# Cross attention scores: from pairs of 64-row products to eight products of 32 rows by 64 columns, two chunks at a time

## The chip, the cores and the metric

The kernel runs on one core of one Trainium2 chip. The metric is the device time of one execution in microseconds (us); the time before is the median of three runs. "PE" is TensorE's matmul side, "PEld" its weight load, DVE is VectorE, ACT ScalarE, POOL GpSimd, SP SyncE.

## The reference

Three residual layers on x (8 batches, 64 rows, 512 features):

```python
x = x + xattn(layernorm(x), ctx)   # 16 heads of 32; ctx is 8 x 1601 x 512
x = x + attn(layernorm(x))         # 8 query heads, one key/value head, causal
x = x + ffn(layernorm(x))          # 2 shared experts, top 2 of 8 routed ones

# xattn, where the change is:
q = query @ Wq.T + bq; k = ctx @ Wk.T + bk; v = ctx @ Wv.T + bv
scores = einsum('bhqd,bhkd->bhqk', q, k) / sqrt(32)
s = where(scores >= 0, scores + 1, 1 / (1 - scores))
out = einsum('bhqk,bhkd->bhqd', s / s.sum(-1), v) @ Wo.T + bo
```

All is computed to fp32 accuracy; the large products split each operand into a high and a low part of a faster type (`wkh`, `wkl`, `cxh`, `cxl`) and add three products.

## The kernel before

Everything is one program, with the order of the work on each engine written out by hand as a loop over slots, and a semaphore for each kind of hand-over. The first 104 slots (`NCH`) are the cross attention: each of the 8 batches has 1601 context rows, cut into 13 chunks (`PER`) of 128 rows, the last of 65; six parts of 256 rows, the last of 321, are the units in which the context is loaded (SP, `load_ctx`), split (ACT `context_hi`, POOL `context_lo`) and turned into keys.

What TensorE does in slot n, in this order (loop at the end of `pe`): steps of the self attention for the two batches just finished, called a tile (t = 0 to 3, steps d = 0 to 14, placed by `slot_of`); `scores(n)`; `attended`, a tile step; `weighted(n - 1)`; `denominators` where a batch is done; two of the four `keys(i, g)` of the next part (one or none in the last slots of a batch); `values(n + 2)`. Keys, values and tile steps share two PSUM banks in turn: `take` waits until the use before the last one has been read out (`proj_read`, counted in the order of `projections()`).

- `scores(n)`, line 692: the query's heads are in `qb`, spread so that 64 rows hold two heads and their columns are zero where the head is the other one. For each g of 4 (four heads) and j of 2 one fp32 product: 64 rows of keys times 128 columns of `qb`, into bank `scb[n % 2][j]`. Two pairs of banks (2 and 3, 4 and 5) take turns, so `scores(n)` waits for the weights of chunk n-2 (`f_dve`).
- ACT turns the scores s into Exp(-Ln(1 + Relu(-s))), two instructions of 512 columns each (lines 1110, 1115, 1119); DVE adds Relu(s) (`weights`, line 1225), which gives the stablemax weight in `tt`, one of `TR` = 3 buffers.
- `weighted(n)`, line 706: 16 fp32 products of 32 columns of values (`va`, one of `VR` = 3 buffers, copied by DVE in `values`, line 1220) and 64 columns of weights, four side by side in four strips of columns.
- POOL adds the weights of each chunk into `dacc` (line 528), from which `denominators` sums over rows.

DVE runs through the same slots in this order: the values copy of the slot before, tile steps, `denominators`, the early `keys` read-outs (line 1212), `weights(n, 0)` and `weights(n, 1)`, the late `keys` read-outs, `normalised`, and in the last slots `weights_split` (line 1320; low parts of the FFN's weights, after ACT's `weights_hi`, line 1068). `weights_hi(1)` and `weights_split(1)` stand at slot 103; the first waits for the last values product (`v_pe`), since its target lies over memory of the cross attention.

From slot 104 on the shared experts run, `shared_up` and `shared_down` (lines 849, 868), then the routed ones (lines 984, 1001). The steps 12 to 14 of tile 2 stand in slots 104 to 106, those of tile 3 begin in slot 106.

## Time and profile before

| | us |
|---|---|
| median of 3 runs (1334.54 to 1336.66) | 1334.65 |
| the profiled execution | 1335.17 |
| its span | 1333.5 |
| PE busy | 1314.2 |
| DVE busy | 657.4 |
| ACT busy | 643.4 |
| POOL busy | 408.6 |
| PE's instructions (matmul records) | 12136 |

The span is what the instructions cover; the execution's own time is 1.67 us more. A matmul's duration in the records overlaps that of its neighbours, since matmuls are pipelined: the distance from start to start is what one costs. Each fp32 product appears as two records of its line (two passes), each split product (keys, values) as one.

### The profile page before, as it was taken

How to read it: one execution, taken by the hardware profiler on the slowest of the kernel's cores; microseconds unless marked ns; L12 is line 12 of the kernel's file. 1: busy time of each engine (PE TensorE's matmuls, PEld its weight loads, DVE VectorE, ACT ScalarE, POOL GpSimd, SP SyncE). 2: the span in 40 equal slices, each digit the busy share in tenths (PEclk: the TensorE clock that was granted, in tenths of full speed). 3: DMA queues.
4: the chain of work that ended last, by engine and by line, in shares of the span. 5: the costliest groups of instructions: out<-in, count | busy, mean ns of one | idle time of the engine just before them, and what ended most of it. 6: DMA issues, size and time to landing. Idle time of an engine off the chain costs nothing.

```text
span 1333.5 us, 28096 instructions
## 1 busy us (share of the span) xinstructions
PE 1314.2 (99%) x12136; PEld 1135.2 (85%) x12136; DVE 657.4 (49%) x979; ACT 643.4 (48%) x1125; POOL 408.6 (31%) x213
## 2 busy tenths in 40 slices
PE   9999999999999999999999999799999999999997
PEld 6888888888788888888889888688988999999896
DVE  5334433534443443443353454656674555455555
ACT  4455545435454543635543644546554354454443
POOL 2344344444354443444444443400013000010000
PEclk9999999999999999999999999899999999999999
DMA  6221111121111111121121130655545389999990
GB/s 215 87 74 32 34 37 33 32 68 49 59 50 33 49 68 49 33 76 32 34 68 65 47 130 21 247 176 186 174 169 185 138 331 337 366 337 335 360 388 34
DMA packets 34868, 174.71 MB, mean 131 GB/s; under 512 B 6154, under 2 KB 8362, under 8 KB 18484
## 3 DMA queue, kind: packets, MB, share of 16 engines
q1 hardware_dynamic: 32996, 168.10, 34.7%
q0 software_dynamic: 1744, 4.76, 1.2%
q8 instruction: 98, 1.61, 0.5%
q14 instruction: 30, 0.25, 0.1%
HBM read 166.78 MB, written 6.06 MB: 130 GB/s over the span
## 4 chain that ended last, share of the span: by engine, by line
PE 96%; DVE 2%; ACT 1%; DMA 1%; POOL 1%; issue 0%; PEldq 0%; SPq 0%; DVEq 0%; PEld 0%; ACTq 0%
PE bank L662 22%; PE bank L674 21%; PE bank L984 11%; PE bank L1001 8%; PE po L868 6%; PE bank L849 6%; PE po L706 4%; PE po L692 4%; PE bank L692 4%; PE bank L766 1%; PE bank L730 1%; PE bank L811 1%; DMA xres<-in_x 1%; PE po L826 1%; PE bank L826 1%; DVE wsl L1320 0%
## 5 line engine op out<-in xcount | busy, mean ns | idle before, releaser
L528 POOL TENSOR_TENSOR xn<-xn,tt 128x1024 f32<-128x1024 f32 x96 | 230.0, 2396 | 406.7 <-DVE tt L1225 406.7
L662 PE MATMUL bank<-cxh,wkh 128*128 128x256 f32 (+1 forms) x752 | 225.9, 300 | 1.1 <-DVE xa L1295 1.1
L1320 DVE TENSOR_TENSOR wsl<-ring,wsh 128x2048 fp32r<-128x2048 f32 x72 | 167.8, 2331 | 114.9 <-ACT wsh L1068 114.7
L662 PE MATMUL bank<-cxl,wkh 128*128 128x256 f32 (+1 forms) x752 | 215.8, 287 | 0.0
L662 PE MATMUL bank<-cxh,wkl 128*128 128x256 f32 (+1 forms) x752 | 214.8, 286 | 0.0
L1212 DVE TENSOR_SCALAR kk<-bank,bkt 128x256 f32<-128x256 f32 (+1 forms) x190 | 93.4, 492 | 241.0 <-PE bank L662 239.9
L674 PE MATMUL bank<-wvh,cxh 128*128 128x512 f32 (+1 forms) x416 | 164.5, 396 | 0.0
L674 PE MATMUL bank<-wvl,cxh 128*128 128x512 f32 (+1 forms) x416 | 163.8, 394 | 0.0
L674 PE MATMUL bank<-wvh,cxl 128*128 128x512 f32 (+1 forms) x416 | 162.7, 391 | 0.0
L1068 ACT CAST wsh<-ring 128x2048 fp32r<-128x2048 f32 x72 | 137.2, 1906 | 47.8 <-PE po L868 24.2
L1110 ACT ACTIVATE tt<-bank 128x512 f32<-128x512 f32 (+1 forms) x104 | 56.5, 595 | 208.6 <-PE bank L692 208.6
L1110 ACT ACTIVATE tt<-po 128x512 f32<-128x512 f32 (+1 forms) x104 | 56.5, 595 | 203.5 <-PE po L692 203.5
L1220 DVE COPY va<-bank 128x512 f32<-128x512 f32 (+1 forms) x104 | 71.7, 689 | 166.9 <-PE bank L674 166.9
L662 PEld LDWEIGHTS bank<-cxh,wkh 128*128 128x128 f32 x752 | 141.7, 188 | 12.8 <-issue 2.9
L984 PEld LDWEIGHTS bank<-xT,ring 128*128 128x128 f32 x1280 | 144.8, 192 | 1.0
L984 PE MATMUL bank<-xT,ring 128*128 128x128 f32 x1280 | 144.8, 275 | 0.0
L662 PEld LDWEIGHTS bank<-cxh,wkl 128*128 128x128 f32 x752 | 142.2, 189 | 0.0
L662 PEld LDWEIGHTS bank<-cxl,wkh 128*128 128x128 f32 x752 | 141.8, 189 | 0.0
L1115 ACT ACTIVATE tt<-tt 128x512 f32<-128x512 f32 (+1 forms) x208 | 119.8, 631 | 0.4
L1119 ACT ACTIVATE tt<-tt 128x512 f32<-128x512 f32 (+1 forms) x208 | 119.3, 627 | 0.0
L514 POOL TENSOR_TENSOR cxl<-ctxt,cxh 128x1024 fp32r<-128x1024 f32 (+1 forms) x47 | 108.5, 2308 | 17.0 <-ACT cxh L1027 17.0
L674 PEld LDWEIGHTS bank<-wvh,cxl 128*128 128x128 f32 (+1 forms) x416 | 76.4, 184 | 20.0
(242 smaller groups left out, 2196.3 us busy)
## 6 DMA issues: line engine op xcount, KB each, us to landing
ring<-in_w SPq DMA_DIRECT2D x112, 1024.0 KB, 6.3
ctxt<-in_ctx SPq DMA_DIRECT2D x40, 512.0 KB, 3.5
ctxt<-in_ctx SPq DMA_DIRECT2D x8, 642.0 KB, 3.9
wqt<-in_wo SPq DMA_DIRECT2D x4, 1024.0 KB, 6.6
wqt<-in_aq SPq DMA_DIRECT2D x4, 1024.0 KB, 7.3
wqt<-in_ap_ SPq DMA_DIRECT2D x4, 1024.0 KB, 6.4
yrows<-K SPq DMA_DIRECT2D x1, 2048.0 KB, 8.9
tt<-in_wk SPq DMA_DIRECT2D x2, 512.0 KB, 5.3
```

The costliest lines, as they stand in the source:

```text
L514: e.tensor_tensor(lo, src, hi.bitcast(F32), ALU.subtract).then_inc(s["cl_pool"], 1)
L528: e.tensor_tensor(dacc[0:kn, y, :], dacc[0:kn, y, :], tt[0:kn, w, :], ALU.add).then_inc(s["da_pool"], 1)
L662: m = e.matmul(dst[:, 0:n], (wkh, wkl)[a][:, c, g * P:(g + 1) * P], (cxh, cxl)[b][:, u, c, 0:n], start=(c == 0 and x_ == 0), stop=(c == 3 ...
L674: m = e.matmul(dst[0:kn, :], (cxh, cxl)[a][:, u, c, k * P:k * P + kn], (wvh, wvl)[b][:, c, :], start=(c == 0 and x_ == 0), stop=(c == 3 an ...
L692: m = e.matmul(scb[n % 2][j][0:kn, P * g:P * g + P], kk[r, u, g, k * P:k * P + kn], qb[r, b % 2, g, :], start=True, stop=True)
L984: m = e.matmul(bank[q % 2][:, P * jj:P * jj + P], ring[slot(un)][:, 512 * c + P * jj:512 * c + P * jj + P], xg[:, y, c, :], start=(c == 0) ...
L1001: m = e.matmul(bank[2][:], h_[:, j, :], w_[r_ % 3][:, 512 * jj:512 * jj + 512], start=(j == 0 and x_ == 0), stop=(j == 15 and x_ == 2))
L1068: e.copy(wsh[m % 3][:], ring[slot(un)][:]).then_inc(s["wh_act"], 1)
L1110: e.activation(tt[0:kn, w, 512 * hb:512 * hb + 512], scb[n % 2][hb][0:kn, :], ACT.Relu, scale=-1.0).then_inc(s["t_act"], 1)
L1115: e.activation(tt[0:kn, w, r], tt[0:kn, w, r], ACT.Ln, bias=1.0).then_inc(s["ln_act"], 1)
L1119: e.activation(tt[0:kn, w, r], tt[0:kn, w, r], ACT.Exp, scale=-1.0).then_inc(s["ex_act"], 1)
L1320: e.tensor_tensor(wsl[m % 3][:], ring[slot(unit_split(m))][:], wsh[m % 3][:].bitcast(F32), ALU.subtract).then_inc(s["wl_dve"], 1)
```

## The change

- `scores` is made of products of 32 rows (one head): the stationary operand is 64 of the chunk's key columns, the moving one the head's 64 query columns straight from `qc`. Eight products (two halves of the chunk, four heads) stand on eight separate tiles of the array; head h writes into bank 2 + h. The last chunk of a batch, 65 rows, is not halved. `qb` with its fill and its copies (`queries`) is gone.
- Chunks go in pairs (`group`): in even slots of a batch both chunks' scores are made, then the weighted sums of the pair before; the 13th chunk is alone. Both chunks' scores share the banks 2 to 5, so a pair waits for the weights of all chunks before it. ACT begins when both chunks of a pair are there (`s_pe`, now one count a chunk). DVE makes the first chunk's weights before the late keys and the second's after them.
- `VR` and `TR` are 4. `tt` holds the heads in the order of the banks, and `weighted` and `denominators` read it so.
- Tile steps stand one slot later; the steps 12 and 13 of tile 2 come to slots 96 and 97. Step 14 stays in slot 104.
- `values` of chunks 101 to 103 move to the slots 101 to 103 (before: 99, 101 and 102). `shared_up(0)` moves from slot 104 to slot 102 and writes into bank 6; `weighted(103)` is first in slot 104.

The diff, without the hunks that only drop `qb`, follow the new banks or move `iota512`:

```diff
@@ -28,8 +28,8 @@
 NPART = NPT * NB
 PER = 13
 NCH = PER * NB
-VR = 3
-TR = 3
+VR = 4
+TR = 4
 NR = 8
 NBLK = 15
 NSH = 16
...
@@ -105,9 +105,9 @@
 
     if t == 3:
         return NCH + 2 + LAST_TILE[d]
-    if t == 2 and d >= 12:
-        return NCH + d - 12
-    return 2 * PER * t + 2 * PER + 5 + (9 if d == 10 else d)
+    if t == 2 and d == 14:
+        return NCH
+    return 2 * PER * t + 2 * PER + 6 + (9 if d == 10 else d)
 
 
 def tile(slot, d):
...
@@ -122,9 +122,30 @@
 
 def values_in(slot):
 
-    if slot + 2 < NCH - 2:
+    if slot + 2 < NCH - 3:
         return slot + 2
-    return slot + 1 if NCH - 2 <= slot + 1 < NCH else None
+    return slot if NCH - 3 <= slot < NCH else None
+
+
+def group(slot):
+
+    if not 0 <= slot < NCH or slot % PER % 2:
+        return ()
+    return (slot, slot + 1) if slot % PER < PER - 1 else (slot,)
+
+
+def group_of(n):
+
+    return group(n) or group(n - 1)
+
+
+def group_before(slot):
+
+    if slot == NCH:
+        return group(NCH - 1)
+    if not group(slot) or slot == 0:
+        return ()
+    return group(slot - 2) or group(slot - 1)
 
 
 def projections():
...
@@ -152,9 +173,10 @@
         def sb(name, shape, dt=F32):
             return st.enter_context(nc.sbuf_tensor(name, shape, dt))
 
-        bank = [st.enter_context(nc.psum_tensor(f"bank{i}", [P, 512], F32)) for i in range(4)]
-        po = st.enter_context(nc.psum_tensor("po", [P, 2048], F32))
-        bank += [po[:, 512 * i:512 * i + 512] for i in range(4)]
+        bank = [st.enter_context(nc.psum_tensor(f"bank{i}", [P, 512], F32)) for i in range(2)]
+        sc = st.enter_context(nc.psum_tensor("sc", [P, 4, 512], F32))
+        bank += [sc[:, i, :] for i in range(4)]
+        bank += [st.enter_context(nc.psum_tensor(f"bank{i}", [P, 512], F32)) for i in range(6, 8)]
 
         ident = sb("ident", [P, P])
         mask = sb("mask", [P, 64])
...
@@ -306,10 +327,13 @@
         pj = [bank[0], bank[1]]
         uses = projections()
         use = {u: n for n, u in enumerate(uses)}
-        scb = (bank[2:4], bank[4:6])
         pob = bank[6:8]
         three = ((0, 0), (0, 1), (1, 0))
 
+        def up_bank(s_):
+
+            return bank[2 + s_ % 2] if s_ else bank[6]
+
         def unit_shared(s_, kind):
 
             return 2 * (s_ // 2) + kind
...
@@ -336,9 +360,13 @@
 
 
 
-        def weights_of(buffer, g, h):
-            c0 = 512 * (h // 2) + 128 * g + 64 * (h % 2)
-            return buffer[:, c0:c0 + 64]
+
+        def score_read(n, kn, hb):
+            c0 = 256 * (n - group_of(n)[0])
+            return sc[0:kn, 2 * hb:2 * hb + 2, c0:c0 + 256]
+
+        def weights_view(n, kn, hb):
+            return tt[0:kn, n % TR, 512 * hb:512 * hb + 512].rearrange("p (h c) -> p h c", h=2)
 
         def ctx_views(i):
             n, u = width(i), i % 2
...
@@ -432,7 +460,6 @@
             e.wait_ge(s["da_pool"], NCH)
             for n in range(5, 8):
                 load_shared(n)
-            store_rows(2)
             for n in range(8, 32):
                 if n == 23:
                     store_rows(3)
...
@@ -677,22 +703,21 @@
 
             def scores(n):
                 i, k, kn = chunk(n)
-                u, b = i % 2, i // NPT
-                if n % PER == 0:
-                    e.wait_ge(s["qb_act"], 4 * b + 4)
+                u, b, c0 = i % 2, i // NPT, 256 * (n - group_of(n)[0])
                 if n >= 2:
-                    e.wait_ge(s["f_dve"], 2 * (n - 2) + 2)
+                    e.wait_ge(s["f_dve"], 2 * group_of(n)[0])
                 else:
                     e.wait_ge(s["q_act"], 4)
                 for g in range(4):
                     if k == 0:
                         e.wait_ge(s["proj_read"], use["k", i, g] + 1)
-                    for j in range(2):
-                        r = slice(64 * j, 64 * j + 64)
-                        m = e.matmul(scb[n % 2][j][0:kn, P * g:P * g + P], kk[r, u, g, k * P:k * P + kn],
-                                     qb[r, b % 2, g, :], start=True, stop=True)
-                        if g == 3:
-                            m.then_inc(s["s_pe"], 1)
+                    for y0, y1 in ((0, 64), (64, P)) if kn == P else ((0, kn),):
+                        for h in range(4):
+                            r = slice(32 * h, 32 * h + 32)
+                            m = e.matmul(sc[y0:y1, h, c0 + 64 * g:c0 + 64 * g + 64],
+                                         kk[r, u, g, k * P + y0:k * P + y1], qc[r, g, 64 * b:64 * b + 64],
+                                         start=True, stop=True)
+                m.then_inc(s["s_pe"], 1)
 
             def weighted(n):
                 kn, b = chunk(n)[2], n // PER
...
@@ -705,8 +730,8 @@
                     for h in range(4):
                         m = e.matmul(pob[b % 2][32 * h:32 * h + 32, 64 * g:64 * g + 64],
                                      va[0:kn, n % VR, P * g + 32 * h:P * g + 32 * h + 32],
-                                     weights_of(tt[0:kn, n % TR, :], g, h), start=(head and g == 0),
-                                     stop=(tail and g == 3), skip_group_check=True)
+                                     tt[0:kn, n % TR, 256 * h + 64 * g:256 * h + 64 * g + 64],
+                                     start=(head and g == 0), stop=(tail and g == 3), skip_group_check=True)
                 m.then_inc(s["p_pe"], 1)
 
             def denominators(b):
...
@@ -835,14 +859,16 @@
                     e.wait_ge(s["wl_dve"], un + 1)
                 if s_ >= 2:
                     e.wait_ge(s["ge_act"], s_ - 1)
+                elif s_ == 1:
+                    e.wait_ge(s["f_dve"], 2 * NCH)
                 else:
-                    e.wait_ge(s["f_dve"], 2 * (NCH - 1))
+                    e.wait_ge(s["cr_dve"], normalised_by(NB - 2))
                 if r == 0:
                     e.wait_ge(s["xl_pool"], 2 + p)
                     if p == 1:
                         e.wait_ge(s["xl_dve"], 1)
                 for i in range(2):
-                    dst, k_ = bank[2 + s_ % 2][:, 256 * i:256 * i + 256], 0
+                    dst, k_ = up_bank(s_)[:, 256 * i:256 * i + 256], 0
                     col = 256 * (s_ % 2) + 128 * i
                     for c in range(4):
                         for w_, x_ in ((wsh, xh), (wsh, xl), (wsl, xh)):
...
@@ -927,21 +953,23 @@
                     turn_third(tile(n, 13))
                 if tile(n, 14) is not None:
                     gate(tile(n, 14))
-                if n < NCH:
-                    scores(n)
+                for m in group(n):
+                    scores(m)
                 if tile(n, 9) is not None:
                     for b in range(2):
                         attended(tile(n, 9), b)
-                if NCH <= n < NCH + 2 * NSH:
+                for m in group_before(n):
+                    weighted(m)
+                if NCH < n < NCH + 2 * NSH:
                     shared_up(n - NCH)
-                if 1 <= n < NCH + 1:
-                    weighted(n - 1)
                 for b in finished(n)[0]:
                     denominators(b)
                 for i, g in early + late:
                     keys(i, g)
                 if values_in(n) is not None:
                     values(values_in(n))
+                if n == NCH - 2:
+                    shared_up(0)
                 if n == PLACE:
                     positions()
                 if n == PLACE + 2:
...
@@ -1056,7 +1075,7 @@
             def split_hi(t):
                 e.wait_ge(s["proj_read"], use["t3", t] + 1)
                 if t == 2:
-                    e.wait_ge(s["d_pe"], NB)
+                    e.wait_ge(s["v_pe"], NCH)
                 e.copy(xh[t // 2][:, :, P * (t % 2):P * (t % 2) + P], xaT[:]).then_inc(s["xh_act"], 1)
 
             def weights_hi(m):
...
@@ -1096,33 +1115,30 @@
                 e.wait_ge(s["q_pe"], g + 1)
                 e.activation(qc[:, g, :], bank[(6, 7, 2, 3)[g]][:], ACT.Identity, bias=bqs[:, g:g + 1],
                              scale=XSCALE).then_inc(s["q_act"], 1)
-            for h in range(4):
-                queries(0, h)
 
             for n in range(NSLOT):
-                if n < NCH:
-                    w, kn = n % TR, chunk(n)[2]
-                    if n >= TR:
-                        e.wait_ge(s["da_pool"], n - TR + 1)
-                        e.wait_ge(s["p_pe"], n - TR + 1)
+                for m in group(n):
+                    kn = chunk(m)[2]
+                    if m >= TR:
+                        e.wait_ge(s["da_pool"], m - TR + 1)
+                        e.wait_ge(s["p_pe"], m - TR + 1)
+                    e.wait_ge(s["s_pe"], group(n)[-1] + 1)
                     for hb in range(2):
-                        e.wait_ge(s["s_pe"], 2 * n + hb + 1)
-                        e.activation(tt[0:kn, w, 512 * hb:512 * hb + 512], scb[n % 2][hb][0:kn, :], ACT.Relu,
+                        e.activation(weights_view(m, kn, hb), score_read(m, kn, hb), ACT.Relu,
                                      scale=-1.0).then_inc(s["t_act"], 1)
+                for m in group(n):
+                    w, kn = m % TR, chunk(m)[2]
                     for hb in range(2):
                         r = slice(512 * hb, 512 * hb + 512)
-                        e.wait_ge(s["t_act"], 2 * n + hb + 1)
+                        e.wait_ge(s["t_act"], 2 * m + hb + 1)
                         e.activation(tt[0:kn, w, r], tt[0:kn, w, r], ACT.Ln, bias=1.0).then_inc(s["ln_act"], 1)
                     for hb in range(2):
                         r = slice(512 * hb, 512 * hb + 512)
-                        e.wait_ge(s["ln_act"], 2 * n + hb + 1)
+                        e.wait_ge(s["ln_act"], 2 * m + hb + 1)
                         e.activation(tt[0:kn, w, r], tt[0:kn, w, r], ACT.Exp, scale=-1.0).then_inc(s["ex_act"], 1)
                 for i in range(2, NPART):
                     if first(i - 1) - 2 == n:
                         context_hi(i)
-                b, h = divmod(n + 5, PER)
-                if 0 < b < NB and h < 4:
-                    queries(b, h)
                 if tile(n, 0) is not None:
                     root(1, tile(n, 0))
                 for half in range(2):
...
@@ -1220,10 +1236,9 @@
                 e.tensor_copy(va[0:kn, n % VR, :], pj[use["v", n] % 2][0:kn, :]).then_inc(s["proj_read"], 1)
 
             def weights(n, hb):
-                kn, w, r = chunk(n)[2], n % TR, slice(512 * hb, 512 * hb + 512)
+                kn, t_ = chunk(n)[2], weights_view(n, chunk(n)[2], hb)
                 e.wait_ge(s["ex_act"], 2 * n + hb + 1)
-                e.scalar_tensor_tensor(tt[0:kn, w, r], scb[n % 2][hb][0:kn, :], 0.0, tt[0:kn, w, r], ALU.max,
-                                       ALU.add).then_inc(s["f_dve"], 1)
+                e.scalar_tensor_tensor(t_, score_read(n, kn, hb), 0.0, t_, ALU.max, ALU.add).then_inc(s["f_dve"], 1)
 
             def stats_of(l, t):
                 e.bn_stats(stats[:, t, :], xres[:, t, :]).then_inc(s["bn_dve"], 1)
...
@@ -1532,11 +1547,14 @@
                     denominators(b)
                 for i, g in early:
                     keys(i, g)
-                if n < NCH:
-                    weights(n, 0)
-                    weights(n, 1)
+                for m in group(n)[:1]:
+                    weights(m, 0)
+                    weights(m, 1)
                 for i, g in late:
                     keys(i, g)
+                for m in group(n)[1:]:
+                    weights(m, 0)
+                    weights(m, 1)
                 for b, g, m in finished(n)[1]:
                     normalised(b, g, m)
 
```

## Rows read from the trace of the kernel before

**Rows 1.** The page: span, its part 1 (busy time, share, instructions) and the granted clock.
```profile
span 1333.5 us, 28096 instructions
PE 1314.2 (99%) x12136; PEld 1135.2 (85%) x12136; DVE 657.4 (49%) x979; ACT 643.4 (48%) x1125; POOL 408.6 (31%) x213
PEclk9999999999999999999999999899999999999999
```

**Rows 2.** The page's part 4: chain of waits, by engine, then by line.
```profile
PE 96%; DVE 2%; ACT 1%; DMA 1%; POOL 1%; issue 0%; PEldq 0%; SPq 0%; DVEq 0%; PEld 0%; ACTq 0%
PE bank L662 22%; PE bank L674 21%; PE bank L984 11%; PE bank L1001 8%; PE po L868 6%; PE bank L849 6%; PE po L706 4%; PE po L692 4%; PE bank L692 4%; PE bank L766 1%; PE bank L730 1%; PE bank L811 1%; DMA xres<-in_x 1%; PE po L826 1%; PE bank L826 1%; DVE wsl L1320 0%
```

**Rows 3.** Busy time in one stretch, all engines; granted clock, DMA share and rate at the end.
```profile
36.80:848.60 811.80, 809.96 (x8829) 688.17 (x8828) 354.60 (x613) 401.42 (x762) 359.61 (x163) 1.00 0.16 53
```

**Rows 4.** Timeline of TensorE in one slot: start, duration, engine, line, names, count.
```profile
401.44 0.40 PE L674 MATMUL bank<-wvl,cxh 128*128 128x512 f32 x1
401.67 0.39 PE L674 MATMUL bank<-wvh,cxl 128*128 128x512 f32 x1
401.99 1.16 PE L692 MATMUL po<-qb,kk 64*128 64x128 f32 x16
403.08 0.65 PE L706 MATMUL po<-tt,va 128*32 128x64 f32 x32
403.67 0.42 PE L662 MATMUL bank<-cxh,wkh 128*128 128x322 f32 x1
403.92 0.31 PE L662 MATMUL bank<-cxl,wkh 128*128 128x322 f32 x1
404.07 0.32 PE L662 MATMUL bank<-cxh,wkl 128*128 128x322 f32 x1
```

**Rows 5.** Groups of instructions by line: fp32 passes of 512, 128 and 8 moving columns.
```profile
L811 PE MATMUL bank<-wqt,xa 128*128 128x512 f32 x32 | 14.4, 592 | 0.0
L766 PE MATMUL bank<-xaT,wqt 128*128 128x128 f32 x128 | 14.9, 275 | 0.0
L743 PE MATMUL bank<-rwt,xaT 128*128 128x8 f32 x32 | 3.8, 246 | 0.0
```

**Rows 6.** Timeline of TensorE: first and last of 24 key products, first values.
```profile
396.40 0.28 PE L662 MATMUL bank<-cxl,wkh 128*128 128x256 f32 x1
396.52 0.28 PE L662 MATMUL bank<-cxh,wkl 128*128 128x256 f32 x1
...
398.89 0.28 PE L662 MATMUL bank<-cxl,wkh 128*128 128x256 f32 x1
399.01 0.28 PE L662 MATMUL bank<-cxh,wkl 128*128 128x256 f32 x1
399.13 0.40 PE L674 MATMUL bank<-wvh,cxh 128*128 128x512 f32 x1
399.37 0.39 PE L674 MATMUL bank<-wvl,cxh 128*128 128x512 f32 x1
```

**Rows 7.** Timeline of ScalarE and VectorE behind the scores of single chunks.
```profile
397.80 1.15 ACT L1119 ACTIVATE tt<-tt 128x512 f32<-128x512 f32 x2
398.45 1.29 DVE L1225 SCALAR_TENSOR_TENSOR tt<-bank,tt 128x512 f32<-128x512 f32 x2
...
402.10 0.69 DVE L1220 COPY va<-bank 128x512 f32<-128x512 f32 x1 [1.96 <-PE bank L674]
403.27 1.09 ACT L1110 ACTIVATE tt<-po 128x512 f32<-128x512 f32 x2 [4.32 <-PE po L692]
404.24 1.15 ACT L1115 ACTIVATE tt<-tt 128x512 f32<-128x512 f32 x2
405.28 1.15 ACT L1119 ACTIVATE tt<-tt 128x512 f32<-128x512 f32 x2
```

**Rows 8.** Groups of instructions of GpSimd: sums of weights, split of the context.
```profile
L528 POOL TENSOR_TENSOR xn<-xn,tt 128x1024 f32<-128x1024 f32 x96 | 230.0, 2396 | 406.7 <-DVE tt L1225 406.7
L514 POOL TENSOR_TENSOR cxl<-ctxt,cxh 128x1024 fp32r<-128x1024 f32 (+1 forms) x47 | 108.5, 2308 | 17.0 <-ACT cxh L1027 17.0
```

**Rows 9.** The page's part 3: the queue that fetches instructions.
```profile
q8 instruction: 98, 1.61, 0.5%
```

**Rows 10.** Timelines and granted clock where the stretch ends.
```profile
847.16 0.28 PE L849 MATMUL bank<-xAh,wsl 128*128 128x256 f32 x1
848.06 0.65 PE L706 MATMUL po<-tt,va 65*32 65x64 f32 x32 [0.62 <-DVE tt L1225]
...
847.02 1.89 ACT L1068 CAST wsh<-ring 128x2048 fp32r<-128x2048 f32 x1
854.83 1.09 PE L750 MATMUL bank<-ident,xa 128*128 128x128 f32 x4 [6.12 <-POOL xa L540]
855.93 0.41 PE L849 MATMUL bank<-xAl,wsh 128*128 128x256 f32 x1
856.15 0.41 PE L849 MATMUL bank<-xAh,wsl 128*128 128x256 f32 x1
859.94 0.28 PE L849 MATMUL bank<-xAh,wsh 128*128 128x256 f32 x1
860.06 0.28 PE L849 MATMUL bank<-xAl,wsh 128*128 128x256 f32 x1
852.80:859.50 6.70, 4.67 (x22) 4.70 (x23) 3.89 (x4) 0.04 (x1) 1.89 (x1) 0.50 1.02 410
853.85 2.28 DVE L1320 TENSOR_TENSOR wsl<-ring,wsh 128x2048 fp32r<-128x2048 f32 x1
```

**Rows 11.** Groups of instructions that the change takes away from ScalarE and GpSimd.
```profile
L1036 ACT COPY qb<-qc 32x256 f32<-32x256 f32 x32 | 12.9, 403 | 0.6
L508 POOL MEMSET qb<- 128x1024 f32 x1 | 1.0, 952 | 0.1
```

More of the change, by code:

```diff
@@ L716, in denominators @@
                     e.wait_ge(s["unit_pool"], 1)
-                dv = dacc[:, b % 2, :].rearrange("p (j g e q) -> p j g e q", j=2, g=4, e=2)
                 for h in range(4):
-                    m = e.matmul(dst[32 * h:32 * h + 32, 0:256], unit[:], dv[:, h // 2, :, h % 2, :], start=True,
-                                 stop=True)
+                    m = e.matmul(dst[32 * h:32 * h + 32, 0:256], unit[:], dacc[:, b % 2, 256 * h:256 * h + 256],
+                                 start=True, stop=True)
                 m.then_inc(s["d_pe"], 1)
@@ L1210, in keys @@
                 if i >= 2 and g == 0:
-                    e.wait_ge(s["s_pe"], 2 * (first(i - 2) + chunks_of(i - 2)))
+                    e.wait_ge(s["s_pe"], first(i - 2) + chunks_of(i - 2))
                 e.tensor_scalar(kk[:, u, g, 0:n], key_bank(i, g)[:, 0:n], bkt[:, g:g + 1], None,
```

18 lines of the change are left out of this document (4 added, 14 removed).

## The prediction

> **What bounds the kernel now.** The page comes first: TensorE is busy for 1314.2 of 1333.5 us at the granted clock 1.0 almost throughout, the other engines for half of the span or less [rows 1]. The profiled execution took 1335.17 us (1.67 beside its span), 0.52 above the median of 1334.65. The chain of waits says the same: PE 96%, the scores (L692) 8%, the weighted sums (L706) 4% [rows 2]. So what counts is TensorE's order of work. The change touches it from 36.8 to 848.6 us, where PE is busy for 809.96 of 811.80 us [rows 3]: there a stall is nearly absent, and every instruction slot saved is time saved unless a new wait eats it.
>
> Next the timeline of one slot [rows 4]. Scores run from 401.99 to 403.08 (1.09 us, 16 passes: each fp32 product is two), weighted sums to 403.67 (0.59 us, 32 passes), then keys. Three times in a slot TensorE changes the form of its tiles, and each change shows as a gap beyond the regular pitch. Values to scores: 0.32 against 0.23 for its neighbours, so 0.09. In the scores the last pass starts 1.16-0.27 = 0.89 after the first; seven later pairs and a late second one make the pitch 0.112, eight pitches 0.90, and 0.19 is left. In the sums 0.65-0.22 = 0.43 lies between first and last start; with the late second group the pitch is 0.056, eight make 0.45, and 0.14 is left. The second key product starts 0.25 after the first against 0.15: 0.10. Together 0.52 us for a round of form changes.
>
> **The change part by part.** (1) *Scores.* Removed per chunk: 8 pairs of passes, 64 rows, 128 columns loaded, 128 moving. Added: 32 products of 32 rows, 64 loaded, 64 moving, in groups of eight on eight separate tiles; 8 groups of passes again (4 head groups, two passes). Nothing in the trace has eight tiles. What sets a pass is read from neighbours: 512 moving columns cost (14.4/4-0.592)/7 = 0.43 us, so 64 cost 0.054; 8 moving columns behind a 128-column load cost (3.8/4-0.246)/7 = 0.10, so a load sets its own pace of about 0.8 ns a column, 64 columns 0.05 [rows 5]. The old pair runs two 128-column loads in 0.112, so loads of different rows run together; the old sums run four 32-column loads in 0.056 where one after another would be 0.10, so loads of different column strips overlap at least by two, and eight tiles need just that [rows 4]. Starts inside a group lie about 7 ns apart (the sums: four tiles, 32 passes in 0.43 us with room left in each 0.056), and eight times 7 is 0.056. All three limits meet at 0.056; I take 0.058 for the group of eight, 0.46 us a chunk against 0.90. The 65-column last chunk of a batch has four tiles and a 65-column load: the same 0.46 against 8 x 0.109. Saving 0.43 x 104 = 45 us. The bounds: 0.056 a group from below (another 2 us won); from above 0.16, if the second passes of four tiles hold back the other four (0.056 behind their first, 0.02 of starts, and all that twice): 1.28 us a chunk, a loss of 0.38 in 96 chunks, 37 us, instead of 45 won.
>
> The Trainium skill's page "TensorE: Matmul & The Clock Gate", section "Part 3: Packing small matmuls", gives 3.07 times for four row tiles and 10.6 times for sixteen, so packing is not free: about 6 times for eight is my estimate between them, 0.075 us a group and 14 us less gained, 1281, still inside case A below. No row here shows row and column tiles together.
>
> (2) *Pairs of chunks.* Each batch of 13 chunks becomes 6 pairs and a single: 48 of 104 rounds of form changes go, 48 x 0.52 = 25 us. This needs no new hardware behaviour; bounds: 16 if the scores' own 0.19 stays with each chunk (0.33 x 48), 25 above, since no other gap exists.
>
> (3) *New waits inside a pair.* The scores of a pair have one set of banks, and ScalarE starts when both chunks are done. Ledger from the start of a pair's scores, no tile step in the slot. PE: scores 2x0.46+0.19 = 1.1, sums 2x0.45+0.14 = 1.0, keys 24 x 0.12 = 2.9 [rows 6], values 12 x 0.23 = 2.8: next slot's keys at 7.9, its second key group at 7.9+1.45 = 9.3. ScalarE: starts 0.39 after the last pass's start (402.88 to 403.27) = 1.4; four Relu at 0.49, then 8 Ln and Exp at 0.52 [rows 7]: 7.6. VectorE's last weights end 0.79 after the last Exp (398.95 to 399.74) = 8.4, then the values copy that queues behind them, 0.69: 9.1 [rows 7]. That copy frees the bank which the second key group takes at 9.3: 0.2 to spare, more where keys are 322 wide. Where an odd slot begins with a tile step that takes a bank itself, the first key group needs that copy: three steps of up to 0.6 us in each of three tiles, I book 3 us. Next scores want the weights at 13.6, there at 8.4. The single chunk: weights at 5.5 (1.0 to ScalarE, 3.1 there, 1.3 on VectorE), the next batch's scores at 6.1. GpSimd's sums, 2.4 us each [rows 8], must be done with a weight buffer before the pair after next writes it, two slots on: room. Its context split waits behind the first of them, until about 11 of 13.6. If ScalarE reads the half banks 10% slower, 0.5 us a pair stands in some 30 pairs: -15 us of the gain. I take 3 for this bound between 0 and 15.
>
> (4) *Instruction supply.* Scores are 128 records a chunk instead of 32, so a pair is a burst of 384 records in about 2 us. The queue of PE's instructions fetches 16.4 KB at a time, 98 packets of 0.005 x 16 x 1333/98 = 1.1 us for 24,272 records, about 250 each [rows 1, 9]: two such reads per pair, one of which falls early in the burst in less than half of the pairs. The only run from an empty queue, the last sums after a wait, keeps full pace from its start: 0.65 us for 32 passes [rows 10]. I book 2 us, bound 15.
>
> (5) *The end of the stretch.* Before: TensorE waits 0.62 for weights at 848.06, then 6.12 for rows of tile 2 at 854.83; the granted clock is 0.50 (1.2 instead of 2.4 GHz) from 852.8 to 859.5, and the 18 products of shared_up(1) in it start 0.21 apart instead of 0.12, some 1.7 lost [rows 10]: 8.4 in all. The change moves tile 2's steps to slots 96 and 97, the 6.12 goes. But values(103) moves to slot 103, and VectorE copies it only in slot 104, behind weights_split(1), which waits for ScalarE's cast, which waits for the last values product. After that product: cast 1.9, split 2.28, copy 0.69 [rows 7, 10], near 5.0; the gate step covers 0.9, so the last sums wait about 4.3. The old wait of 6.12 brought the clock down, this shorter one may (1.7, taken by half). shared_up(0), 2.9 us, moves ahead of the last scores, whose banks must be free by then. Net 8.4-4.3-0.9 = 3.2 won; I take 3, bounds 0 and 6.
>
> (6) *Removed with it.* Eight batches of four copies of 0.40 us on ScalarE (L1036) and one GpSimd fill [rows 11] lie beside PE's work; without them nothing starts sooner. The weights of the later stage load by the same waits, all moved ahead; from 848.6 on nothing else changes.
>
> Sum: 45+25-3-2+3 = 68, 1335.17-68 = 1267.2; against the median 1266.6. I say 1267.
>
> A rule against the change is on the Trainium skill's page "TensorE: Matmul & The Clock Gate", section "Wait — 56ns, not 53.3ns?": with one kind of decode the sequencer spends about 62 ns on each matmul. By it I estimate 64 x 0.062 = 4 us a chunk for the scores, far slower than before. The trace disagrees: the sums start 32 passes in 0.43 us [rows 4]; so it gets no chance.
>
> **The rivals.** *A, forecast:* full packing, 1256 to 1282. Chance 0.56. *B, supply or issue sets the burst:* records leave more slowly than one in 3.5 ns; the sums have shown 64 in 0.44, 7 ns each. At 5 to 7 ns a group of eight costs 0.08 to 0.11, scores 0.64 to 0.88 a chunk: 18 to 44 us of the 45 lost, 1285 to 1311. For it: no burst over 96 records in the trace; against: full pace from an empty queue. Chance 0.24. *C, packing gives nothing* (two strips of the same rows load one after the other): 8 x 0.112, only parts 2 and 5: 1335-25-3+5 = 1312, up to 1325 with part 3's upper bound. Against: four strips in 0.056. Chance 0.07. *D, slower:* passes interleave by four tiles at most, so the first four tiles' second passes hold the other four back: 0.16 a group, 8 x 0.16 = 1.28 a chunk, +0.38 x 96 = +37, less 25 and 3 won, plus 5 of waits: about 1349. It decides from 0.145 a group on, where 8 x 0.033 x 96 eats 25. For it: no row shows more than four interleaved; against: pairs and fours follow their tiles exactly. Chance 0.10. Same within 0.2% (what a measurement can tell): 0.03.
>
> **From the cases.** Faster 0.56+0.24+0.07 = 0.87, same 0.03, slower 0.10. The range reaches from A's lower end to the upper part of B, 1256 to 1307; A alone has 1256 to 1282.
>
> **What would show it.** Scores' line: 16 groups of eight, first to last start near 0.9 us for a pair, ScalarE's first Relu 1.4 after the scores' start; if 1.3 or more, B; 1.8, C; 2.5, D. Rounds of form changes: 56. A wait of key products for the values copy in the odd slots over 0.3 us proves part 3 too small; a gap inside the burst without a releaser is part 4; a wait of the last sums for va near 4.3 us is part 5. The prediction is wrong if the stretch up to the last sums doesn't shorten by 60 to 75 us.

## The result, and the profile after

The changed kernel takes 1373.42 us (median of 4 runs, 1370.99 to 1376.40), the kernel before beside it 1334.60: ratio 1.029, interval 1.027 to 1.031. It is 38.8 us slower, where I forecast 67 us faster. The scores did get cheaper. TensorE lost more than that standing still.

The page of the changed kernel answers first: span, busy time, granted clock (in tenths, 40 slices) and the instruction queue (packets, MB, share of 16 engines), then the chain of waits.

```profile
span 1369.3 us, 37532 instructions
...
PE 1285.3 (94%) x16872; PEld 1121.7 (82%) x16872; DVE 655.4 (48%) x979; ACT 624.1 (46%) x1093; POOL 406.6 (30%) x212
...
PEclk9999999999999999999999999999999999999999
...
q8 instruction: 135, 2.21, 0.7%
...
PE 86%; issue 5%; DVE 4%; ACT 3%; DMA 1%; PEldq 0%; SPq 0%; DVEq 0%; PEld 0%; ACTq 0%
```

PE is busy for 28.9 us less than in [rows 1] and yet the span is 35.8 us longer; "issue", 0% in [rows 2], is 5% of the chain. The stretch that the change touches, now to the end of its last sums (window, busy time and count of PE, PEld, DVE, ACT, POOL, then clock, DMA share, GB/s):

```profile
36.80:893.00 856.20, 783.83 (x13555) 677.44 (x13544) 356.68 (x616) 388.68 (x739) 365.95 (x165) 0.98 0.15 52
```

72 us without a product, against 2 in [rows 3]. The waits of TensorE (what waited, for whom, total, times, longest) name them:

```profile
PE bank L731 <- issue: 42.4, 22, 4.5
PE bank L688 <- DVE va L1236: 13.3, 11, 1.6
PE bank L688 <- issue: 10.1, 9, 2.7
PE bank L731 <- DVE va L1236: 4.6, 1, 4.6
...
PE bank L743 <- issue: 1.0, 1, 1.0
```

L731 are the weighted sums, L688 the keys, L717 the scores, L743 the denominators. The three lines of "issue" add up to 53.5 us, in which nothing that the profile shows is late: I call such a wait a stop, and a row of short instructions without a pause a burst. One stop, in the timeline of TensorE behind a pair's scores:

```profile
179.36 1.59 PE L717 MATMUL sc<-qc,kk 32*64 32x64 f32 x128
180.88 1.08 PE L731 MATMUL bank<-tt,va 128*32 128x64 f32 x58
183.38 0.31 PE L731 MATMUL bank<-tt,va 128*32 128x64 f32 x6 [1.42 <-issue]
183.63 0.39 PE L688 MATMUL bank<-cxh,wkh 128*128 128x256 f32 x1
```

The sums are 32 products of two passes each. 58 of the 64 passes run at full pace, then TensorE stands for 1.42 us and does the last 6. The DMA view of 180 to 184 us (40 slices of 0.1 us, then the queue's packets, MB, share) has one packet, and it fetches instructions:

```profile
GB/s 0 0 0 0 0 0 0 0 164 0 0 0 0 0 0 0 0 0 0 0 0 0 0 0 0 0 0 0 0 0 0 0 0 0 0 0 0 0 0 0
DMA packets 1, 0.02 MB, mean 4 GB/s; under 512 B 0, under 2 KB 0, under 8 KB 0
...
q8 instruction: 1, 0.02, 2.0%
```

It starts at 180.8 and takes 0.02 x 16 x 4 = 1.3 us, to about 182.1; TensorE resumes 1.3 us later. It is so at every stop: the trace has 30 of more than 0.5 us, and each ends 2.2 to 3.0 us after the start of an instruction packet. The next two stops end at 199.32 and 216.04. From one end to the next:

```profile
183.37:199.31 15.94, 14.08 (x254) 12.44 (x254) 5.62 (x10) 7.60 (x15) 7.46 (x3) 1.00 0.10 35
199.31:216.03 16.72, 15.58 (x254) 13.95 (x254) 5.98 (x10) 6.31 (x13) 6.93 (x3) 1.00 0.11 34
```

254 passes and 254 loads, and with four semaphore instructions of TensorE that the trace has beside them 512, both times: two blocks of 256. The packets say the same: the changed kernel has 9,472 passes and loads more and 37 packets more than the one before, 256 for each, and 2.21 MB in 135 packets is 16.4 KB each. The stops keep to one place in the block, since a pair's two slots, where no tile step stands in them, are 512 instructions long. The Trainium skill gives the block on its page "Advanced Engine Details and Errata", section "ISA Cache": a cache line is 16 KB, 256 instructions. The trace agrees, by the counts above.

### The profile page after: what moved, and what is told of

Its sections match the earlier page's. It is cut to its first block, busy times and chain, and to the rows that moved or that the text cites. A ratio compares the mean times of both kernels' runs of the same rounds, so it can differ in the third digit from the quotient of the medians.

```text
span 1369.3 us, 37532 instructions
## 1 busy us (share of the span) xinstructions
PE 1285.3 (94%) x16872; PEld 1121.7 (82%) x16872; DVE 655.4 (48%) x979; ACT 624.1 (46%) x1093; POOL 406.6 (30%) x212
## 3 DMA queue, kind: packets, MB, share of 16 engines
q8 instruction: 135, 2.21, 0.7%
## 4 chain that ended last, share of the span: by engine, by line
PE 86%; issue 5%; DVE 4%; ACT 3%; DMA 1%; PEldq 0%; SPq 0%; DVEq 0%; PEld 0%; ACTq 0%
PE bank L688 19%; PE bank L700 19%; PE bank L1012 10%; PE sc L1029 8%; PE sc L875 6%; PE sc L717 6%; PE bank L731 4%; PE sc L894 3%; PE bank L894 3%; DVE tt L1241 2%; PE bank L790 1%; PE bank L754 1%; PE bank L835 1%; ACT tt L1134 1%; ACT tt L1127 1%
## 5 line engine op out<-in xcount | busy, mean ns | idle before, releaser
L1127 ACT ACTIVATE tt<-sc 128x512 f32<-128x512 f32 (+1 forms) x208 | 107.7, 602 | 453.8 <-PE sc L717 453.8
L688 PE MATMUL bank<-cxh,wkh 128*128 128x256 f32 (+1 forms) x752 | 225.9, 300 | 19.0 <-DVE va L1236 13.3
L688 PE MATMUL bank<-cxh,wkl 128*128 128x256 f32 (+1 forms) x752 | 217.4, 289 | 3.7 <-issue 3.7
L688 PE MATMUL bank<-cxl,wkh 128*128 128x256 f32 (+1 forms) x752 | 218.2, 290 | 1.7 <-issue 1.5
L688 PEld LDWEIGHTS bank<-cxh,wkh 128*128 128x128 f32 x752 | 144.4, 192 | 30.7 <-DVE va L1236 16.1
L688 PEld LDWEIGHTS bank<-cxl,wkh 128*128 128x128 f32 x752 | 144.5, 192 | 5.6 <-issue 4.2
L688 PEld LDWEIGHTS bank<-cxh,wkl 128*128 128x128 f32 x752 | 144.7, 192 | 2.9 <-issue 2.8
L1241 DVE SCALAR_TENSOR_TENSOR tt<-sc,tt 128x512 f32<-128x512 f32 (+1 forms) x208 | 133.2, 682 | 25.4 <-ACT tt L1138 24.9
L1134 ACT ACTIVATE tt<-tt 128x512 f32<-128x512 f32 (+1 forms) x208 | 121.3, 647 | 0.0
L1138 ACT ACTIVATE tt<-tt 128x512 f32<-128x512 f32 (+1 forms) x208 | 121.1, 644 | 0.0
L731 PE MATMUL bank<-tt,va 128*32 128x64 f32 (+1 forms) x3328 | 65.2, 223 | 47.0 <-issue 42.4
```

The source lines that it names most:

```text
L688: m = e.matmul(dst[:, 0:n], (wkh, wkl)[a][:, c, g * P:(g + 1) * P], (cxh, cxl)[b][:, u, c, 0:n], start=(c == 0 and x_ == 0), stop=(c == 3 ...
L731: m = e.matmul(pob[b % 2][32 * h:32 * h + 32, 64 * g:64 * g + 64], va[0:kn, n % VR, P * g + 32 * h:P * g + 32 * h + 32], tt[0:kn, n % TR, ...
L1127: e.activation(weights_view(m, kn, hb), score_read(m, kn, hb), ACT.Relu, scale=-1.0).then_inc(s["t_act"], 1)
L1134: e.activation(tt[0:kn, w, r], tt[0:kn, w, r], ACT.Ln, bias=1.0).then_inc(s["ln_act"], 1)
L1138: e.activation(tt[0:kn, w, r], tt[0:kn, w, r], ACT.Exp, scale=-1.0).then_inc(s["ex_act"], 1)
L1241: e.scalar_tensor_tensor(t_, score_read(n, kn, hb), 0.0, t_, ALU.max, ALU.add).then_inc(s["f_dve"], 1)
```

## The experiments

Times are medians; ratios are to the kernel before on the same chip, with their intervals. In the expectations "issue" is the wait above, a "gap" is a stop, and a "record" is one instruction in the trace, a pass or a load. Code is cut to what matters; "..." marks what is left out.

**e1.** The pair's sums go behind the slot's key products, so that 256 and 128 instructions run in a row and not 384.

```
-                for m in group_before(n):
-                    weighted(m)
...
                 for i, g in early + late:
                     keys(i, g)
+                for m in group_before(n):
+                    weighted(m)
```

> The changed kernel with one thing moved: a pair's weighted sums stand behind the slot's key products, so that at most 256 short records follow each other instead of 384. Same work. Theory F (the engine's instructions come in blocks of 256; a block's fetch takes some 3.4 us from the crossing of the block before to its use, and a pair's burst eats 320 records in less): the gaps at L731 (some 52 us in all) and most of those in L688 behind it go, one more change of form per pair costs 0.1 to 0.2 us, 8 us in all: 1300 to 1320 us. Rival S (the sums wait for a semaphore, weights or values of the pair before): those were ready long before, moving changes nothing but the form change: 1375 to 1385. Rival D (the array needs longer between forms): 1380.

1327.88 us, ratio 0.9945 (0.9929 to 0.9962). 45.5 us less for a mere change of order: the issue waits fell from 53.5 to 12.4 us. It is 8 above the expected band, in which none of the stops in the sums was to be left. Five stay, 2.2 to 3.2 us each, and all five stand behind heavy DMA traffic (see the long stops, below); 9.5 us of waits for values stay too.

```profile
PE bank L731 <- issue: 12.4, 5, 3.2
PE bank L688 <- DVE va L1236: 9.5, 11, 1.5
```

**e2.** Pairs with the old score products (128 columns, 64 rows), and with them `qb` and its copies, in one buffer: pairing without the new products.

```
-                    for y0, y1 in ((0, 64), (64, P)) if kn == P else ((0, kn),):
-                        for h in range(4):
-                            r = slice(32 * h, 32 * h + 32)
...
+                    for j in range(2):
+                        r = slice(64 * j, 64 * j + 64)
+                        m = e.matmul(sc[0:kn, 2 * c + j, P * g:P * g + P], kk[r, u, g, k * P:k * P + kn],
+                                     qb[r, g, :], start=True, stop=True)
```

> Pairs of chunks as in the changed kernel, but the scores in their old form: 64 rows, 128 columns, 32 records a chunk, copies of the queries as before (one buffer). Tells pairing from the new form. Theory F: a burst is 192 records, no gap at a block's end; 48 rounds of form changes go (25 us), the end of the stretch as in the changed kernel, the copies' queue costs 1 to 3: 1305 to 1318 us. Rival P (pairing itself loses by waits of key products for the values copy, ScalarE and VectorE): above 1335.

1332.72 us, ratio 0.9988 (0.9978 to 0.9998): nearly nothing, and between the two expectations. From the first start of each run to the first start of the next line, summed over the timeline, the scores fell from 112.9 to 103.2 us, 9.7, and the sums by 6.6 (0.137 in each of 48 pairs, which take 1.031 against 2 x 0.584). It has no issue wait in its list of waits. What eats the 16 us is the wait of the keys (L694 here), absent before:

```profile
PE bank L694 <- DVE va L1257: 15.7, 13, 1.8
PE bank L737 <- DVE va L1257: 4.6, 1, 4.6
```

**e3.** The new score products, chunk by chunk: part 1 alone (with the new order at the end). `group_before` gives the one chunk before, and with one set of banks each chunk's scores wait for the weights of the chunk before.

```
 def group(slot):
-    if not 0 <= slot < NCH or slot % PER % 2:
-        return ()
-    return (slot, slot + 1) if slot % PER < PER - 1 else (slot,)
+    return (slot,) if 0 <= slot < NCH else ()
```

> The new form of the scores, chunk by chunk in every slot as before the change, one set of banks (a chunk waits for the weights of the one before). Tells the form from pairing. Theory F: bursts of 192 records, no gap at a block's end; a chunk's scores take 0.81 us to the next line instead of 1.09, the 65-column ones 0.63 instead of 1.05: 96 x 0.28 + 8 x 0.42 = 30 won: 1300 to 1315 us. Rival A (the array is slow with eight tiles): first to last start of a chunk 0.69 and more, and gaps stay: above 1330.

1310.85 us, ratio 0.9823 (0.9806 to 0.9839): faster than both kernels, and no issue wait at all. A burst is 128 + 64 = 192 instructions here. Scores take 86.0 us instead of 112.9.

**e4, e5, e6.** The changed kernel with 64, 80 or 40 products more at its very start, of one pass each: all later instructions move by 128, 160 or 80 places against the edges of the blocks, and nothing else changes. Here e4; e5 has 140 and e6 has 100.

```
-            warm(60, bank[7])
+            warm(124, bank[7])
```

> The changed kernel with 64 more dummy products (128 records) at its start, before the first keys, and nothing else. Theory F: every gap stands at the same number of instruction modulo 256 as before, counted from the start, so 128 records earlier in the work: other pairs stall, the sum of the gaps stays within a third, and the time is 1373 plus 4 to 6 for the dummies, plus or minus 15. Rival S: the same pairs stall at the same place of the work, and their number modulo 256 moves by 128.

> The changed kernel with 80 products more at its start, so 160 TensorE instructions more ahead of all the rest; nothing else. Theory F (a block of 256 instructions is asked for when TensorE is some 360 instructions ahead of its first one and is there 3.6 us later; where the 300 in between run in less, TensorE stands): I laid this over the trace of the changed kernel with its stops taken out, and moved it. It gives 44.7 us of stops for the changed kernel, 13.9 for the shift of 128 (traces: 53.5 and 22.6 put down to issue), 8.1 for this shift, the lowest of all sixteen tried. Expected: issue waits of 13 to 20 us, time 1322 to 1334, 1328 likeliest. Rival (the shift of 128 won by another cause, such as the longer start): no less than 1334 and issue waits of 22 or more.

> The changed kernel with 40 products more at its start: 80 instructions. Theory F: the same sum gives 31.0 us of stops, 13.7 less than unshifted; with 1.2 us for the products 1359 (1352 to 1365), issue waits about 40 us in the trace. Rival (any shift does): about 1335, as with 128.

1334.85 us (ratio 1.0002, 0.9992 to 1.0013), 1332.51 (0.9983, 0.9971 to 0.9996) and 1347.50 (1.0088, 1.0064 to 1.0111). The issue waits of e5, then of e6:

```profile
PE bank L731 <- issue: 11.3, 6, 4.5
...
PE bank L688 <- issue: 4.4, 4, 2.1
...
PE bank L700 <- issue: 1.3, 1, 1.3
```
```profile
PE bank L731 <- issue: 33.2, 20, 5.1
...
PE bank L688 <- issue: 1.4, 2, 0.9
```

So issue waits of 53.5, 34.6, 22.6 and 17.0 us go with 1373.4, 1347.5, 1334.9 and 1332.5 us. Work added at the start takes 26 to 41 us off the time, and how much depends on where the block's edges then fall. My expectation for e4 had missed: I thought the burst would be cut at any phase. For e5 and e6 I then took the trace's own start times without the stops and let each block be asked for some 360 instructions ahead of its first and be there 3.6 us later; e5 came inside its band, e6 5 us below it. The rule, fitted to one trace, has the shape right and not the size: it gave 44.7, 31.0, 13.9 and 8.1 us of stops where the traces have 53.5, 34.6, 22.6 and 17.0. It leaves out the long stops (below).

**e7.** e3 with its scores cut in two runs of 32 passes, the previous chunk's sums between them: does the slow second half of a score run belong to its products, or to the length of the run?

```
                 for m in group(n):
-                    scores(m)
+                    scores(m, range(0, 2))
+                for m in group_before(n):
+                    weighted(m)
+                for m in group(n):
+                    scores(m, range(2, 4))
...
-                for m in group_before(n):
-                    weighted(m)
```

> The variant with the new scores chunk by chunk (1310.85 us), its 64 score products cut into two runs of 32, head groups 0 and 1 ahead of the previous chunk's sums and 2 and 3 behind them. In that variant the first 36 products started within 0.29 us and the other 28 took 0.36, and a run of scores took 0.843 us to the next line; the sums, 0.56 us for 64 instructions, are slower than the instruction supply of about 5.4 ns each. Theory F: the supply catches up by some 40 instructions during the sums, so each half runs at its fast pace (0.23 us) and pays one switch more (0.13 to 0.17 us): 0.05 to 0.15 us less a chunk, 1295 to 1306. Rival (the slow second half is no matter of supply, or a switch costs more than the supply): no gain or up to 15 us more, 1311 to 1326.

1316.51 us, ratio 0.9857 (0.9841 to 0.9874): 5.7 above e3, where 5 to 16 less were expected; the rival's band holds it. The question is answered all the same. One slot of e3, then one of e7:

```profile
408.03 0.92 PE L711 MATMUL sc<-qc,kk 32*64 32x64 f32 x64
408.87 0.65 PE L725 MATMUL bank<-tt,va 128*32 128x64 f32 x32
409.46 0.39 PE L682 MATMUL bank<-cxh,wkh 128*128 128x256 f32 x1
```
```profile
408.01 0.49 PE L711 MATMUL sc<-qc,kk 32*64 32x64 f32 x32
408.43 0.65 PE L726 MATMUL bank<-tt,va 128*32 128x64 f32 x32
409.01 0.49 PE L711 MATMUL sc<-qc,kk 32*64 32x64 f32 x32
409.43 0.38 PE L682 MATMUL bank<-cxh,wkh 128*128 128x256 f32 x1
```

With a pass of 0.23 us, 32 passes start within 0.26 us both times, and 64 without a break within 0.69 and not 0.52. The same e3 slot in stretches that grow by 0.06 us, then the whole run (length, busy time and passes begun, the same of loads, clock, DMA share, GB/s):

```profile
408.03:408.25 0.22, 0.22 (x24) 0.22 (x32) 1.00 0.00 0
408.03:408.31 0.28, 0.28 (x32) 0.28 (x33) 1.00 0.00 0
408.03:408.37 0.34, 0.34 (x33) 0.34 (x34) 1.00 0.00 0
408.03:408.73 0.70, 0.70 (x64) 0.70 (x64) 1.00 0.00 0
```

The first group of eight takes 0.107 us, the next ones start 0.058 apart, and behind the 33rd pass the pace breaks, in each of e3's 96 full chunks at the same pass. From there a long run falls to some 5.5 ns an instruction, load or pass. In e7 the same products run at full pace once the sums stand ahead of them, so it is the length of the run and not the products. That a stock of instructions in TensorE runs out there is argued from this: another store that fills or empties within a run would look alike, and no run separates them. The cut wins nothing, since the sums in between cost one more change of tiles, 0.15 us: two runs of 0.42 are what one of 0.84 was. The profiled spans, 1310.3 and 1316.7, differ by 6.4 us, and 4.8 of these are in its list of waits: against e3, 1.7 more for `xa` at the denominators, 1.6 for `cxl` at the keys, 1.0 for weights at the scores and 0.5 at the last sums. By line, 3.0 us of the growth stand at the self-attention's products, which come behind the second half here.

**e8.** e2 with VectorE's normalisation of a finished batch behind the copy of the values: what is missing in the ledger of part 3?

```
                 if n and values_in(n - 1) is not None:
                     values(values_in(n - 1))
+                for b, g, m in finished(n - 1)[1]:
+                    normalised(b, g, m)
...
-                for b, g, m in finished(n)[1]:
-                    normalised(b, g, m)
```

> The variant with pairs and the old scores (1332.7 us), with VectorE's normalisation of a finished batch (2.7 to 3.7 us) behind the copy of the values instead of ahead of it. There the key products waited 15.7 us for that copy, 13 times. Theory F (the pair's later weights and the normalisation together hold the copy up): at least 11 of the 15.7 go, 1318 to 1323. Rival (VectorE has no room: the wait moves to the next slot or to the sums): 1328 or more.

1321.17 us, ratio 0.9898 (0.9881 to 0.9914): 11.6 us less than e2, and the waits of the keys for values went from 15.7 to 3.7. The row that I had missed, in e2, VectorE behind a pair's last weights:

```profile
458.93 1.29 DVE L1262 SCALAR_TENSOR_TENSOR tt<-sc,tt 128x512 f32<-128x512 f32 x2 [0.40 <-ACT tt L1156]
460.13 0.94 DVE L1382 RECIPROCAL xT<-xT 128x128 f32<-128x128 f32 x1
461.11 0.29 DVE L1387 TENSOR_TENSOR xT<-bank,xT 128x128 f32<-128x128 f32 x1
461.44 1.49 DVE L1389 TENSOR_TENSOR xT<-xT,bvt 128x128 f32<-128x128 f32 x1
462.85 0.68 DVE L1257 COPY va<-bank 128x512 f32<-128x512 f32 x1
```

**e9.** e3 with the split of the second block of expert weights (4.4 us) behind the copy of the last values: part 5.

```
+                if n == NCH:
+                    weights_split(1)
...
-                if n == NCH - 1:
-                    weights_split(1)
```

> The variant with the new scores chunk by chunk, with one step on VectorE moved: the split of the second block of expert weights (4.38 us) goes behind the copy of the last chunk's values, which waited for it while TensorE stood 6.27 us ahead of the last sums. Theory F: that copy is then over 1 us behind the last value product, the wait shrinks to about 1.1 us and the clock, at half speed behind the wait, stays up: 5 to 7 us less, 1304 to 1306. Rival: the split is then late for the first product that reads it, or the wait was another's: 1309 to 1312.

1306.77 us, ratio 0.9794 (0.9776 to 0.9812): 4.1 less than e3, where 5 to 7 were expected (the two profiled spans, 1310.3 and 1303.4, differ by 6.9). The wait of 6.27 us ahead of the last sums is 0.48. A new one has come, and it is the rival's: the moved split holds up VectorE's next step, `hl` (L1340), which the first `shared_down` product needs.

```profile
826.17 4.45 DVE L1329 TENSOR_TENSOR wsl<-ring,wsh 128x2048 fp32r<-128x2048 f32 x1 [0.81 <-ACT wsh L1081]
...
831.07 0.69 DVE L1340 SCALAR_TENSOR_TENSOR hl<-hr,hh 128x512 fp32r<-128x512 f32 x1
...
831.86 0.76 PE L888 MATMUL sc<-wsh,hh 128*128 128x512 f32 x1 [2.20 <-issue]
```

The view puts these 2.20 us down to "issue", but `hl` ends at 831.76, 0.1 us before the product, and the instruction packet before it started 10.9 us earlier. The same wait, 2.0 to 2.2 us, is in e10, e11 and e12, which have this edit, and in no other run.

**e10.** The changed kernel with e5's shift, e8's and e9's edits together.

> The changed kernel with three edits: the 80 products more at its start (shift of 160 instructions), the normalisation behind the copy of the values, the split of the second expert weights behind the copy of the last values. With the shift alone it took 1332.5 us, with 17.0 us of issue waits in the trace, 14.5 of key products for the copies of values and 4.6 of the last sums. If these causes add up: 10 to 12 and 4 us less, 1313 to 1320, still above the chunk by chunk variant (1306.8), since the issue waits stay. Rival (they don't add up, the pair costs something else): 1324 or more.

1318.55 us, ratio 0.9876 (0.9859 to 0.9892). The causes add up, 14.0 us below e5. 18.2 us of issue waits stay in the sums, the keys and the values, 12.6 of them in three stops.

**e11.** The control: e9 with e4's shift, `warm(124, bank[7])`.

> A control: the chunk by chunk variant with the later split (1306.8 us) and 64 products more at its start, the shift of 128 instructions that took 38.6 us off the changed kernel. Its slots have 192 instructions in a row and no stop. Theory F: nothing but the products' own 2 us, 1306 to 1311. Rival (the longer start or the shift helps by itself): 1300 or less.

1308.43 us, ratio 0.9807 (0.9791 to 0.9823), 1.7 above e9 and inside the spread of e9's own runs (1304.84 to 1308.83). Where no burst outruns the supply, the same shift wins nothing.

**e12.** e9 with the sums alone in pairs: every second slot has 256 instructions in a row.

```
 def group_before(slot):
-    return group(slot - 1)
+    if slot == NCH:
+        return pair(NCH - 1)
+    if not pair(slot) or slot == 0:
+        return ()
+    return pair(slot - 2) or pair(slot - 1)
```

(`pair` is the changed kernel's `group`.)

> The chunk by chunk variant with the later split (1306.8 us), with the sums alone in pairs: a slot in two has 64 score products and behind them 64 of sums, 256 instructions in a row, the other 64 score products alone. The switch saved is 0.137 us a pair in the traces (1.168 for two runs of sums against 1.031), 6.6 us over 48. Theory F (up to about 300 instructions in a row are safe): no stop in the bursts, 1299 to 1303. Rival (256 in a row already stop it, by 0.5 to 1.5 us each time that the block's edge falls there): 1308 to 1325, with issue waits at the sums or the keys.

1302.23 us, ratio 0.9754 (0.9738 to 0.9771): the best version, 32.2 us faster than before, and 4.5 below e9 of the 6.6 that the saved changes of tiles are worth. Its stretch to 840 us, and the first of its list of waits (keys; the other issue wait, 2.0 us, is e9's). 1.8 us is a stop of the old kind, behind DMA engines that were 94% busy: 256 in a row are not quite safe.

```profile
36.80:840.00 803.20, 796.25 (x13684) 679.84 (x13682) 366.44 (x629) 398.04 (x745) 366.47 (x165) 1.00 0.18 63
...
PE bank L691 <- issue: 2.3, 2, 1.8
```

## Why the prediction was wrong

The step that failed is part 4, instruction supply, booked at 2 us with a bound of 15; it was 53.5 us of waits. I counted that a block comes every 250 instructions and priced the packet's own 1.1 us, as if the rest of the delivery could be hidden in any case. The prediction's own sign for it, a gap inside the burst without a releaser, is what the trace shows. In the stop at 183.38 the packet starts 1.4 us after the first pass of the scores; 58 passes of sums later its block is the one wanted, and from the packet's start to TensorE's next pass it takes 2.6 us. A pair's 384 instructions leave in 2.4 us. So the reserve is smaller than a delivery wherever the block's edge falls into the late part of the burst, and that is where it fell in most pairs. The argument from an empty queue, 64 instructions at full pace in [rows 10], says nothing on this: it is a burst of 64 instructions, not of 384, and doesn't test the block behind it. e1, e3, e4, e5, e6 and e11 show this cause: with shorter bursts the stops go (e3) or all but five do (e1); with the same bursts at another phase they shrink to between a third and two thirds; and the same shift without long bursts changes next to nothing.

The long stops belong to it: they too end 2.2 to 2.5 us after a packet's start, but the packet starts late. Of the four of 4.2 to 4.5 us, three came with a load of 1 MB of weights, a context load and a store in flight, the fourth with two loads of 1 MB. In 394 to 397 us, in which TensorE would have needed its block, the DMA engines were busy and had no instruction packet; it came in the next microsecond:

```profile
q1 hardware_dynamic: 169, 1.01, 95.1%
...
q8 instruction: 1, 0.02, 5.8%
```

Behind it, key products ran 0.21 us apart, at the granted clock 0.50 (1.2 of 2.4 GHz), for 4 us:

```profile
399.37 0.43 PE L731 MATMUL bank<-tt,va 128*32 128x64 f32 x5 [4.43 <-issue]
399.70:403.70 4.00, 4.00 (x20) 3.97 (x19) 1.00 (x3) 2.21 (x4) 0.00 (x0) 0.50 0.02 4
```

The other traces bear it out. Of the 23 stops of 2 us and more in this kernel, e1, e4, e5, e6 and e10 (e9's wait apart), 22 have other packets on the DMA engines for 70% or more of the 3 us before the instruction packet starts, and one for 54%; of this kernel's 25 shorter stops one has. All that is left in e1 and e12 is of this kind. So what long bursts cost depends on the traffic beside them too. That the traffic held the packets up is still read from traces: no run took the traffic away.

Point by point. *Part 1, 45 us:* the pitch of 0.058 a group holds from the second to the fourth group only; the first takes 0.107, and over a pair's 16 the mean is 0.086. That is the pace of rival B. Alone (e3) it gave 27 us. *Part 2, 25 us:* 9.7 and 6.6 us in e2, the lower bound of 16 that I had named: the scores' 0.19 stays with each chunk, and so I chose the wrong end. *Part 3, 3 us:* the keys' waits for values were 13.3 us, near the upper bound. The ledger was right for an ordinary slot and left out the slots with a normalisation, which e8 prices at 11.6 us. *Part 5, 3 us:* the last sums waited 4.6 us for the values (predicted 4.3), behind the split as foretold; that mechanism was right. With the old wait gone (6.3) and the new one come (4.9 by the sums below), the part won 1.4 us. e9 shows that most of the wait was needless: without it e3 is 4.1 us shorter, and 2.2 us come back at `shared_down`. *Part 6* costs nothing, as forecast.

The ledger of before against after, by the same sums over the timeline as in e2 (the old wait of 6.3 at the end counted apart, in us): scores -34.5; sums -6.5 by pairs and +52.5 by stops, of which 42.4 are issue; keys +23.1 (13.3 for values, 10.1 issue); the end -6.3 and +4.9; first steps of a tile and denominators +5.8; the rest about -3. Together +36 of the span's 35.8.

Rival D, the slower case with its 1349, named interleaved passes at 0.16 a group. It did not occur: groups of eight started 0.058 apart at best and 0.086 on average. The result was slower by the supply of instructions, which I had put into part 4 with its bound of 15 and into rival B, capped at 1311.

## What to carry to other kernels

Packing small products multiplies instructions: count those in a row, not only their time. Here 192 in a row behind slow products cost no stop, 256 cost two (e12) or five (e1), all beside heavy DMA traffic, and 384 in 2.4 us cost 0.6 to 2 us wherever the 256-instruction block's edge fell badly, and up to 4.5 us beside that traffic. Breaking the burst, or keeping it to a block, was worth more than the switches of tiles that pairing saved. When "issue" is in the chain of waits, look for the instruction queue's packets beside the stops: here each stop of more than 0.5 us ended 2.2 to 3.0 us after the start of one, and the one "issue" wait that did not was a wait for VectorE (e9). Then shift the program by a few dozen instructions: a time that moves by per cents, with no other edit, points at the supply.

## What the runs showed of the hardware

TensorE's instructions came in blocks of 256, one packet of 16.4 KB each. From a packet's start to TensorE's next pass it took 2.6 us at 183.38, of which 1.3 are the packet, and 2.2 to 3.0 us in all 30 stops. Behind a change of tiles 33 passes with their loads start within 0.29 us, from the second group on at some 3.6 ns an instruction; after that each takes some 5.5 ns (e3; e7 shows that it is the length of the run). Eight tiles of 32 rows and 64 columns started a group each 0.058 us within these 33, so tiles that differ in rows and columns overlap there. And phase matters: 128 instructions of padding took 38.6 us off a kernel with bursts of 384, and changed one with bursts of 192 by 1.7 us, within its spread.
